# A causal mask in attention: added by matmuls, or by VectorE's instruction that finds a score maximum

## The reference, cut to what matters

```python
q = (x @ wq_w.T + wq_b).reshape(b, t, 32, 32)      # b, t, D = 8, 512, 1024
k1, v1 = (x @ wk_w.T + wk_b), (x @ wv_w.T + wv_b)  # one key/value head of 32
scores = jnp.einsum('bqhd,bkd->bhqk', q, k1) / jnp.sqrt(jnp.float32(32))
scores = jnp.where(causal, scores, -jnp.inf)       # causal: tril, t x t
weights = jax.nn.softmax(scores, axis=-1)
attn = jnp.einsum('bhqk,bkd->bqhd', weights, v1).reshape(b, t, 1024)
return attn @ wo_w.T + wo_b
```

## Time and profile before

| what | value |
|---|---|
| median of 3 runs | 2995.59 us (2989.72 to 2997.83) |
| span of the profiled execution | 2999.3 us |
| PE (TensorE) busy | 2801.1 us, 93% |
| DVE (VectorE) busy | 1620.4 us, 54% |
| ACT (ScalarE) busy | 1159.1 us, 39% |
| POOL (GpSimd) busy | 945.7 us, 32% |

### The profile page before, as it was taken

One profiled execution on the slowest core, in us unless ns is written; L12 is line 12 of the kernel. 1 busy time (PEld: TensorE's weight loads), 2 busy tenths in 40 slices (PEclk: granted clock), 3 DMA queues, 4 the chain that ended last, 5 costly groups with the idle time before them and its releaser, 6 DMA issues. The chain is left out here.

```text
span 2999.3 us, 41858 instructions
## 1 busy us (share of the span) xinstructions
PE 2801.1 (93%) x15808; PEld 2116.6 (71%) x15808; DVE 1620.4 (54%) x2960; ACT 1159.1 (39%) x2509; POOL 945.7 (32%) x1460
## 2 busy tenths in 40 slices
PE   5888999999999999999999987999999999999988
PEld 3666767767777677676776565787878787878766
DVE  3453464553744645536444346666666666666653
ACT  3664365462744645627445012222222222222220
POOL 2333122121221222212213044444454444444422
PEclk8889999999999999999999888999999999999989
DMA  5765545544545454445354510010101010201011
GB/s 155 197 162 151 169 106 150 126 117 127 137 93 166 107 160 124 104 148 127 82 151 147 174 46 1 2 56 2 56 5 52 5 53 2 56 2 56 1 28 29
DMA packets 103626, 272.29 MB, mean 91 GB/s; under 512 B 12122, under 2 KB 23514, under 8 KB 101122
## 3 DMA queue, kind: packets, MB, share of 16 engines
q1 hardware_dynamic: 102706, 269.55, 33.2%
q10 hardware_dynamic: 720, 0.07, 0.0%
HBM read 168.40 MB, written 50.33 MB: 73 GB/s over the span
## 5 line engine op out<-in xcount | busy, mean ns | idle before, releaser
L659 DVE TENSOR_REDUCE top<-ps_attn 128x1 fp32r<-128x512 f32 (+3 forms) x704 | 441.0, 639 | 466.4 <-PE ps_attn L834 460.5
L471 POOL TENSOR_SCALAR_AFFINE_SELECT pt<-pt 128x512 f32<-128x512 f32 x256 | 163.3, 649 | 954.6 <-ACT pt L558 954.6
L558 ACT ACTIVATE pt<-ps_attn 128x512 f32<-128x512 f32 (+1 forms) x704 | 381.3, 559 | 137.3 <-PE ps_attn L861 137.0
L1555 PE MATMUL ps_mixer<-m_w_hi,m_xt_hi 128*128 128x512 f32 x1024 | 423.5, 414 | 1.6 <-DVE m_xt_lo L1337 1.6
L572 ACT ACTIVATE spent<-ps_attn,top 128x512 f32<-128x512 f32 (+1 forms) x512 | 325.4, 636 | 240.1 <-DVE top L659 238.3
L1557 PE MATMUL ps_mixer<-m_w_lo,m_xt_hi 128*128 128x512 f32 x1024 | 407.9, 398 | 0.0
L1556 PE MATMUL ps_mixer<-m_w_hi,m_xt_lo 128*128 128x512 f32 x1024 | 407.9, 398 | 0.0
L861 PE MATMUL ps_attn<-q_stack,k_stack 97*128 97x512 f32 (+3 forms) x1024 | 298.8, 352 | 38.5 <-DMA q_stack<-top_rows 28.5
L831 PE MATMUL ps_attn<-k_stack,q_stack 96*128 96x512 f32 (+3 forms) x1024 | 304.9, 350 | 28.4 <-DMA q_stack<-q_lo 14.5
L1237 ACT CAST m_xt_hi<-ps_mixer 128x512 fp32r<-128x512 f32 x192 | 104.2, 589 | 494.1 <-PE ps_mixer L1550 494.0
L831 PEld LDWEIGHTS ps_attn<-k_stack,q_stack 96*128 96x128 f32 x1024 | 176.1, 195 | 105.2 <-ACT spent L572 49.9
(11 more groups left out here) (216 smaller groups left out, 5114.3 us busy)
## 6 DMA issues: line engine op xcount, KB each, us to landing
xr<-in_a_x SPq DMA_DIRECT2D x64, 512.0 KB, 6.7
q_stack<-q_hi SPq DMA_DIRECT2D x128, 256.0 KB, 5.6
wq_hi<-wq_split SPq DMA_DIRECT2D x56, 512.0 KB, 3.9
wq_lo<-wq_split SPq DMA_DIRECT2D x56, 512.0 KB, 4.6
q_stack<-q_lo SPq DMA_DIRECT2D x64, 256.0 KB, 6.8
wo_hi<-wo_split SPq DMA_DIRECT2D x8, 2048.0 KB, 8.4
wo_lo<-wo_split SPq DMA_DIRECT2D x8, 2048.0 KB, 12.8
x<-xr SPq DMA_DIRECT2D x32, 512.0 KB, 2.8
```

What stands on the lines that cost most here:

```text
L558: nc.scalar.activation(pt[k][:, heads[0]:heads[0] + len(heads), :].rearrange("p j t -> p (j t)"), ps[:, ST0 + n % 2, 0:width * len(heads)] ...
L659: nc.vector.tensor_reduce(out, ps[:, S0 + n % 2, 0:width * len(heads)].rearrange("p (j k) -> p j k", k=width), AX.X, ALU.min).then_inc(s_u ...
L1555: nc.tensor.matmul(out, a_hi, b_hi, start=first, stop=False)
```

## The change

The mask products go. `tops` becomes one `tensor_tensor_reduce` per head: it adds a mask to the head's scores in the bank, writes the sum back into the bank, and gives the minimum, in full fp32, to `top_exact`. So units 8 and 9 have two instructions and unit 10 has four, 16 per group where 11 were. The mask tile is 512 wide, zero but for its last 128 columns. Two small VectorE instructions follow: `round_tops` copies `top_exact` into `top` (rounding), and `tops_turned` now waits for it; `shift_diff` takes the difference between the rounded and the exact values of the last two tiles. ScalarE takes exp of that (`shift_scale`), and VectorE multiplies `den` by it before the reciprocal (`den_invert`, now behind `divide` and `x_low`). `row_sum` takes the exact bias and writes its elements over the bank. In the setup, `mask` needs a memset besides, two parameters pass through `pt[1]` instead of `spent`, and some semaphores are merged, in the mixer too.

```diff
-                    nc.scalar.activation(spent[:, 0:width], ps[:, S0 + n % 2, 0:width], ACT.Exp, scale=-1.0,
-                                         bias=top[:, j * TILES + i:j * TILES + i + 1].bitcast(F32),
+                    nc.scalar.activation(ps[:, S0 + n % 2, 0:width], ps[:, S0 + n % 2, 0:width], ACT.Exp, scale=-1.0,
+                                         bias=top_exact[:, j, i:i + 1],
                                          accum_out=den[:, i - (TILES - SUM_TILES), j:j + 1]).then_inc(den_done, 1)
+
+                def shift_scale(G):
+                    act.wait_ge(diff_done, G + 1)
+                    if G:
+                        act.wait_ge(den_scaled, G)
+                    nc.scalar.activation(top_scale[:, :, :], top_diff[:, :, :], ACT.Exp).then_inc(scale_done, 1)
...
-                        if u == 0 and G:
-                            dve.wait_ge(topt_ready, G)
-                        out = top[:, 0:GH * TILES].rearrange("p (j i) -> p j i", i=TILES)[:, heads[0]:heads[0] + len(heads), i]
-                        nc.vector.tensor_reduce(out, ps[:, S0 + n % 2, 0:width * len(heads)].rearrange("p (j k) -> p j k", k=width),
-                                                AX.X, ALU.min).then_inc(s_used, 1)
+                        for m, j in enumerate(heads):
+                            own = ps[:, S0 + n % 2, m * width:(m + 1) * width]
+                            found = nc.vector.tensor_tensor_reduce(own, own, mask[:, T - width:T], 1.0, FAR, ALU.add, ALU.min,
+                                                                   top_exact[:, j, i:i + 1])
+                        found.then_inc(s_used, 1)
+
+                def round_tops(G):
+                    dve.wait_ge(s_used, U * (G + 1))
+                    if G:
+                        dve.wait_ge(topt_ready, G)
+                    nc.vector.tensor_copy(top[:, 0:GH * TILES].rearrange("p (j i) -> p j i", i=TILES), top_exact[:, :, :]
+                                          ).then_inc(top_done, 1)
+
+                def shift_diff(G):
+                    dve.wait_ge(top_done, G + 1)
+                    if G:
+                        dve.wait_ge(scale_done, G)
+                    rounded = top[:, 0:GH * TILES].bitcast(F32).rearrange("p (j i) -> p i j", i=TILES)[:, TILES - SUM_TILES:TILES, :]
+                    exact = top_exact[:, :, TILES - SUM_TILES:TILES].rearrange("p j i -> p i j")
+                    nc.vector.tensor_tensor(top_diff[:, :, :], rounded, exact, ALU.subtract).then_inc(diff_done, 1)
...
                     dve.wait_ge(den_done, SUMMED * (G + 1))
+                    dve.wait_ge(scale_done, G + 1)
+                    nc.vector.tensor_tensor(den[:, :, :], den[:, :, :], top_scale[:, :, :], ALU.mult).then_inc(den_scaled, 1)
+                    dve.wait_ge(den_scaled, G + 1)
...
                         tops(M + 1, (9, 10))
-                        den_invert(M + 1)
+                        round_tops(M + 1)
+                        shift_diff(M + 1)
                     if first is not None:
                         x_low(first, 1)
                     if inside(M - 1):
                         divide(M - 1)
+                    if inside(M + 1):
+                        den_invert(M + 1)
...
-                    diagonal = bank.rearrange("p (j k) -> p j k", k=width)[:, :, i * P:width]
-                    nc.tensor.matmul(diagonal, ident_r[:, :], causal_r[:, None, :].to_broadcast([P, len(heads), P]),
-                                     start=False, stop=True).then_inc(s_ready, 1)
+                    mm.then_inc(s_ready, 1)
 
                 def tops_turned(G):
-                    pe.wait_ge(s_used, U * (G + 1))
+                    pe.wait_ge(top_done, G + 1)
```

More of the change, by code:

```diff
@@ L14 @@
 U8 = mybir.dt.uint8
+FAR = 3.0e38
 PENDING = []
@@ L172, in attention_blocks @@
         ones = sb("ones", [P, HEAD])
-        top = sb("top", [P, P], F32R)
+        top, top_exact = sb("top", [P, P], F32R), sb("top_exact", [P, GH, TILES])
+        top_diff, top_scale = sb("top_diff", [P, SUM_TILES, GH]), sb("top_scale", [P, SUM_TILES, GH])
         top_rows = sb("top_rows", [GH * TILES, P], F32R)
@@ L179, in attention_blocks @@
         bq_sb, bkv_sb, kvs_sb, bkv_scaled = sb("bq_sb", [P, CH]), sb("bkv_sb", [P, 1]), sb("kvs_sb", [P, 1]), sb("bkv_scaled", [P, 1])
-        ident_r, causal_r = sb("ident_r", [P, P], F32R), sb("causal_r", [P, P], F32R)
-        spent, den, den_inv = sb("spent", [P, T]), sb("den", [P, 2, GH]), sb("den_inv", [P, 2, 2, GH])
-        identb_sb, causal_sb = spent[:, 0:P // 2].bitcast(BF16), spent[:, P // 2:P].bitcast(BF16)
+        ident_r, mask = sb("ident_r", [P, P], F32R), sb("mask", [P, T])
+        den, den_inv = sb("den", [P, 2, GH]), sb("den_inv", [P, 2, 2, GH])
+        identb_sb, causal_sb = pt[1][:, 0, 0:P // 2].bitcast(BF16), pt[1][:, 0, P // 2:P].bitcast(BF16)
         ps = ctx.enter_context(nc.psum_tensor("ps_attn", [P, 8, HALF], F32))
@@ L251, in _ @@
                 pool.wait_ge(params_in, 5 * DMA)
-                nc.gpsimd.tensor_scalar(kvs_sb[0:KROWS, :], kvs_sb[0:KROWS, :], -1.0, None, ALU.mult).then_inc(kvs_turned, 1)
-                pool.wait_ge(kvs_turned, 1)
-                nc.gpsimd.tensor_tensor(bkv_scaled[:, :], bkv_sb[:, :], kvs_sb[:, :], ALU.mult).then_inc(bkv_ready, 1)
+                nc.gpsimd.tensor_scalar(kvs_sb[0:KROWS, :], kvs_sb[0:KROWS, :], -1.0, None, ALU.mult).then_inc(setup_done, 1)
+                pool.wait_ge(setup_done, 4)
+                nc.gpsimd.tensor_tensor(bkv_scaled[:, :], bkv_sb[:, :], kvs_sb[:, :], ALU.mult).then_inc(setup_done, 1)
                 inv_sqrt(pool, 0, 2)
@@ L267, in _ @@
                 wq_high(act, 0)
-                act.wait_ge(bkv_ready, 1)
+                act.wait_ge(setup_done, 5)
                 act.wait_ge(params_in, 5 * DMA)
@@ L278, in _ @@
                 nc.vector.tensor_copy(ident_r[:, :], identb_sb).then_inc(mask_done, 1)
-                nc.vector.tensor_scalar(causal_r[:, :], causal_sb, -1.0, None, ALU.mult).then_inc(mask_done, 1)
+                nc.vector.memset(mask[:, 0:T - P], 0.0).then_inc(mask_done, 1)
+                nc.vector.tensor_scalar(mask[:, T - P:T], causal_sb, -1.0, None, ALU.mult).then_inc(mask_done, 1)
                 normalise(dve, 0, 1)
@@ L290, in _ @@
             def _(pe):
-                pe.wait_ge(mask_done, 3)
+                pe.wait_ge(mask_done, 4)
                 pe.wait_ge(setup_done, 3)
@@ L637, in _ @@
                             x_high(first, 1)
+                    if inside(M + 1):
+                        shift_scale(M + 1)
                     for G in finishes(M):
@@ L830, in scores @@
                     for m, j in enumerate(heads):
-                        nc.tensor.matmul(bank[:, m * width:(m + 1) * width], q_stack[0:KROWS, G % 3, j, i * P:(i + 1) * P],
-                                         k_stack[0:KROWS, b % 2, 0:width], start=(m == 0), stop=False)
-                    diagonal = bank.rearrange("p (j k) -> p j k", k=width)[:, :, i * P:width]
-                    nc.tensor.matmul(diagonal, ident_r[:, :], causal_r[:, None, :].to_broadcast([P, len(heads), P]),
-                                     start=False, stop=True).then_inc(s_ready, 1)
+                        mm = nc.tensor.matmul(bank[:, m * width:(m + 1) * width], q_stack[0:KROWS, G % 3, j, i * P:(i + 1) * P],
+                                              k_stack[0:KROWS, b % 2, 0:width], start=(m == 0), stop=(m == len(heads) - 1))
+                    mm.then_inc(s_ready, 1)
                 def tops_turned(G):
-                    pe.wait_ge(s_used, U * (G + 1))
+                    pe.wait_ge(top_done, G + 1)
                     b, g = divmod(G, GROUPS)
@@ L1065, in mixer_blocks @@
         delta_ready, sum_done, whi_done, wlo_done = sem("delta_ready"), sem("sum_done"), sem("whi_done"), sem("wlo_done")
-        setup, small, gate_exp, a_exp = sem("setup"), sem("small"), sem("gate_exp"), sem("a_exp")
+        setup, small, param_exp = sem("setup"), sem("small"), sem("param_exp")
         x_in = [[sem(f"x_in_{n}_{t}") for t in range(TILES)] for n in range(2)]
```

11 lines of the change are left out of this document (6 added, 5 removed).

## The result

The changed kernel takes 3051.56 us (median of 4 runs, 3048.61 to 3056.65), the kernel before 2993.98 beside it: ratio 1.019, 95% interval 1.0171 to 1.0209. It is slower by 58 us, where 2992 was forecast and 3035 was the end of the range. The profiled execution has a span of 3051.1 us against 2999.3, so 51.8 us are to be found in the traces.

What follows compares the result with a forecast made beforehand. TensorE sets the pace, but VectorE's end has only 0.5 us margin in plain steps. Terms 4 - 14 + 5 - 4 + 2 + 3 + 0.3 = -4 us, from a median of 2995.6 to 2992; range 2950 to 3035.

Steps and rivals of the forecast that it cites:

- The rounding copy: `round_tops` on VectorE between the last maximum and the turn: a signal and 0.19 us.
- the later `divide`: shift_diff puts 0.2 us ahead of divide, finish_high and the turned rows' copy; no cost was booked for it.
- the later `den_invert`: Later in VectorE's order, delays spread on GpSimd by 0.8 us: nothing; steps like 38 were booked at -4 us.
- TensorE's clock: Read as granted in full in both step windows; no term for a change of it.
- rival 4: VectorE's end doesn't bind, masks come out whole: 60 to 75 us in 64 steps, about 2925; 8%.
- The gain from unit 0 to unit 6: Mask products of units 0 to 5 leaving TensorE before unit 6: 0.68 us a step.
- d: What one new VectorE instruction takes beyond the reduce of its width: 0.11 us; 0.01 of it is 4.6 us.
- rival 1: The minimum rides along in the same instruction, d from 0 to 0.07: 2947 to 2974 us; 25%.
- the forecast 6.84: Plain step's tail from unit 6's score matmul to the turn's start, in us; 6.05 before, so 0.79 later.
- +0.15: Booked in each of 27 plain steps, +4 us: the turn 0.79 later against 0.68 gained ahead of unit 6.
- Rival 2: The new instruction has a dearer start too, d 0.16 to 0.2: +19 to +37 us, about 3020; 22%.
- rival 3: Reading and writing one bank in the same instruction halves its rate: +3.3 us in some 45 steps, about 3150; 5%.

Runs made afterwards that it cites:

- experiment 1: The kernel before without the mask products (L834) and with nothing in their place, the mask left out: 2952.9 us, ratio 0.9848.
- A: The changed kernel with the whole change, timed beside the kernel before: 3051.56 us, ratio 1.019.
- 10: Changed kernel with the new instruction, exact maxima turned, no rounding, difference or scale product on VectorE, sums' correction left out: 2979.61 us, ratio 0.9953.
- 4: A with exact maxima turned, rounded by ScalarE's row copy; round_tops, shift_diff, den_invert behind divide and the keys, shift_scale behind finish_high: 2982.75 us, ratio 0.9953.
- 8: A with shift_diff and den_invert both behind divide and behind kv_in, the rounding copy alone left ahead of the turn: 3006.73 us, ratio 1.0044.
- experiment 7: A with kv_in (keys and values) ahead of den_invert in VectorE's order: 3018.5 us, ratio 1.0092.
- experiment 6: A with one edit, shift_diff behind divide in VectorE's order: 3035.74 us, ratio 1.014.
- B: The kernel before the change, timed beside all the others: 2993.98 us beside A, 2993.5 to 2995.3 beside the experiments.
- experiment 11: The version turning exact maxima (2982.8 us), with unit 10 as in B, one mask product and one reduce for four heads: 2965.71 us, ratio 0.9921.
- experiment 3: A with three 512-wide TensorE products before the wait for the rounding copy, in steps without output: 3056.12 us, ratio 1.0194.

## Why the prediction was wrong

Four steps of the forecast failed. The rounding copy was priced at under a third of its usual length; the later `divide` and the later `den_invert` were booked at nothing; and TensorE's clock was left out. The masks and the instruction itself were both priced too high, one in the change's favour and one against it.

The kernels form a chain between experiment 1 and A, by their medians:

| kernel | us | step |
|---|---|---|
| 1: no masks, nothing in their place | 2952.9 | |
| 10: the new instruction | 2979.6 | +26.7 |
| 4: the correction, off the path | 2982.8 | +3.1 |
| 8: the rounded maxima turned, copy ahead of the turn | 3006.7 | +24.0 |
| 7: `shift_diff` ahead of `divide` | 3018.5 | +11.8 |
| A: `den_invert` ahead of the keys | 3051.6 | +33.1 |

Steps 4 and 8 differ in the place of `shift_scale` too. The first step holds the small rest of the change as well. The 3.1 is within the error, the 11.8 just outside it (16 by experiment 6). Each step contains what the clock made of it.

- **The masks.** Priced at up to 1.45 us a step and 60 to 75 in all (rival 4); in B they are worth 42 in all. The gain from unit 0 to unit 6 was put at 0.68 and was 0.55. Too high, but not the cause of the miss.
- **The instruction.** d was taken as 0.11. From start to start it is 0.25 for 128 columns and 0.38 for 256, against the 0.19 and 0.33 that I had worked out for a reduce: d is 0.05 to 0.06, inside rival 1. The small record is there, as the rule of two instructions in the Trainium skill (VectorE: DVE Perf Modes, Two Vector instructions with no wait between them) had it; only most of it is overlapped.
- **The rounding copy.** Priced at 0.19; it is 0.17 alone and 0.65 in most steps. This step of the sum failed. The two errors hide each other: 10 x 0.055 less, 0.46 more, and unit 6 to the turn is 6.77 against the forecast 6.84. A tail that came out right was right by accident.
- **`divide` against the turn.** `shift_diff` was booked at nothing: its 0.2 ahead of `divide` was followed only to ScalarE and to the shift DMA. I never looked at who else reads `att_done`. It is `weigh_first`, the first instruction behind the turn, and no term was booked for it. `divide` had started 0.49 ahead of the turn; now VectorE's own copy releases the turn, and `divide` stands behind that copy. This is the step that failed most in plain steps at the full clock. Turn to unit 0 grew by 0.61: 0.22 of it go when `shift_diff` moves (experiments 6 and 8). The other 0.39 stay; only with the exact maxima turned and unit 10 as in B do they shrink to 0.09 (unit 0 at 1.81, experiment 11). Step 51 is then +0.72 - 0.55 + 0.61 = +0.78. Steps like 37 grow by the same 0.6. Plain steps behind an output step don't meet it, since VectorE is long done there (1.66 both before and after): they are +0.15, just as forecast, though with two terms that were each off (0.72 for 0.79, 0.55 for 0.68). For the same reason the output steps with M mod 8 = 1 gained 0.71, and those with 0 did not: 39.30 at the full clock against 39.34, and 40.9 in those with a slow stretch.
- **`den_invert` later: "nothing".** Wrong, and the largest term by the chain. In steps like 38 it stood ahead of the keys, behind a wait for ScalarE. I asked who needs `den_inv`, and not what is queued behind the waiting instruction on VectorE. -4 was booked, +17.4 came, and +13.6 in the steps behind.
- **The clock.** The forecast took the full clock of the two windows and had no term for a change of it. Half clock went from 24 to 116 us. The 27 plain steps grew by 32.5 us; at the full clock they would have grown by some 13 (7 times 0.15, 14 times 0.79, 6 times 0.15, the last from experiment 7), so some 19, by this estimate, are the clock's. Nearly all of the 13.6 of the steps behind the keys is of this kind: experiment 7 brings back 2.2 us in each of them, with the gap and the slow stretch both gone.
- **The rivals.** Rival 2 had the right sign and a time 30 us too low, for a reason that isn't there; rival 3 is excluded by 702 ns for 512 columns. None had the order of VectorE's work as its mechanism.

Open: the 6.6 us behind attention, where all these kernels lie between some 1287 and 1301 with the same work; and why the clock is granted less. That the slow stretches follow from the gaps is not shown: experiment 7 removed a gap and the stretch behind it went, experiment 3 filled some gaps and gained nothing.

## What to carry to other kernels

When instructions are added to an engine near its end, list for each position every later instruction on that queue with its reader, and cost the shift at each reader. An engine can have more than one end that counts, and a reader of the second can be the next iteration's first instruction. A step that waits for another engine belongs behind everything that doesn't need it. And price a small instruction by its rows beside its neighbours on GpSimd, not alone.

## What the runs showed of the hardware

- A copy of 16 elements on VectorE takes 0.17 us, or until 0.03 us behind the end of a GpSimd instruction that was running when it started (45 of 64 in A, 0.65 in most); the keys' copy takes 0.42 or 1.34. A reduce of the same data is never held (169 to 171 ns in 64), a subtraction of two SBUF tiles is (0.43 instead of 0.17). The Trainium skill (SBUF — State Buffer, SBUF: two separate sides) has a pair of ports that VectorE and GpSimd lock in turn, for VectorE's copies in a fast mode and for two SBUF inputs; the rows agree.
- A VectorE minimum with an element output reads and writes the same bank at 702 ns for 512 columns, the plain reduce is 685, and its accumulator read of 142 ns overlaps the next instruction.
- A step granted 0.91 of TensorE's clock in the mean took 19.44 us, one of the same kind at 1.00 took 17.91. The granted clock stayed at 1.00 (2.4 GHz) for 1.4 us without a matmul, and the stretch behind it was granted 0.50 (1.2 GHz), across the turn at 1079.70:

```profile
1076.60:1078.00 1.40, 0.00 (x0) 0.00 (x0) 1.37 (x3) 0.17 (x1) 1.40 (x2) 1.00 0.00 0
1078.10:1084.90 6.80, 5.20 (x22) 2.50 (x23) 2.19 (x5) 0.73 (x2) 0.64 (x2) 0.50 0.31 95
```
- ScalarE's sum of 512 columns with its elements written over the bank takes 662 ns against 688 into SBUF in the kernel before.
